# Mamba stage of a decoder layer: the side work of the next item placed at other states, half of delta times x on VectorE

## The reference, cut to what matters

```
xz = x @ in_w.T;  xb, z = split(xz)                       # 512 channels each
xb = silu(causal_conv(xb, 4 taps) + cb)
delta, Bm, Cm = split(xb @ xp_w.T)                         # ranks 16, 16, 16
delta = softplus(delta @ dt_w.T + dt_b)
mi  = delta[..., None] * Bm[:, :, None, :] * xb[..., None]
v_t = 0.6 * v_{t-1} + mi_t                                 # per channel and state
h_t = exp(delta_t * -exp(a_log)) * h_{t-1} + v_t
y   = sum over the 16 states of h * Cm;  y = (y + dp * xb) * silu(z)
x   = x + y @ out_w.T
```

## Time and profile before

| | |
|---|---|
| median of three runs | 1560.0 us |
| profiled execution | 1560.36 us, of which the span of the instructions is 1558.9 us |
| Mamba block (first to last scan) | 80.5 to 982.0 us of the span |
| TensorE, ScalarE, VectorE, GpSimd busy, share of the span | 88%, 58%, 68%, 59% |

### The profile page before, as it was taken

How to read it: one execution, slowest core, us unless ns; L and a number is a source line. 1 busy time by engine, 2 the same in 40 slices (tenths; PEclk the granted TensorE clock), 3 DMA queues, 4 the chain that set the end, 5 groups by cost and what they waited for, 6 DMA issues and landing times.

```text
span 1558.9 us, 46788 instructions
## 1 busy us (share of the span) xinstructions
PE 1372.9 (88%) x20442; PEld 975.9 (63%) x20442; DVE 1066.0 (68%) x1347; ACT 908.8 (58%) x1365; POOL 921.2 (59%) x802
## 2 busy tenths in 40 slices
PE   4679799999899899899899886878989887999997
PEld 2357577777677677667677775533444343499996
DVE  4189898798689688788788786577676771422223
ACT  3658567777767667767666765116555655434440
POOL 1159888989979969969969986530303000035541
PEclk8689999999999999999999998969999999999999
DMA  4102212222212212221221344370414100612225
GB/s 134 49 28 85 83 65 75 85 83 96 84 71 84 84 57 84 84 72 69 87 81 70 138 128 125 76 149 1 84 39 85 24 1 15 264 47 69 68 66 179
DMA packets 41497, 127.26 MB, mean 82 GB/s; under 512 B 8784, under 2 KB 21584, under 8 KB 32848
## 3 DMA queue, kind: packets, MB, share of 16 engines
q1 hardware_dynamic: 34736, 108.27, 21.4%
q0 software_dynamic: 6048, 14.95, 3.6%
q10 hardware_dynamic: 512, 1.05, 0.4%
HBM read 97.90 MB, written 9.57 MB: 69 GB/s over the span
## 4 chain that ended last, share of the span: by engine, by line
PE 59%; DVE 20%; issue 10%; ACT 4%; POOL 4%; DMA 2%; DVEq 0%; SPq 0%; ACTq 0%; POOLq 0%
PE psum L631 12%; DVE hst L783 9%; PE psum L610 8%; PE psum L1710 4%; PE psum L1722 4%; PE psum L1298 4%; PE psum L515 3%; POOL hst L987 3%; PE psum L601 3%; DVE overlay L679 2%; PE psum L1280 2%; DVE w_early L783 2%; PE psum L1652 2%; PE psum L1264 2%; DVE nmax L1419 2%
## 5 line engine op out<-in xcount | busy, mean ns | idle before, releaser
L987 POOL TENSOR_TENSOR hst<-hst,cb 128x512 f32<-128x512 f32 x399 | 513.5, 1306 | 125.7 <-DVE hst L783 110.3
L783 DVE TENSOR_TENSOR_SCAN hst<-dA,psum 128x512 f32<-128x512 f32 x399 | 467.1, 1204 | 140.7 <-PE psum L631 140.4
L610 PE MATMUL psum<-ident,hst 128*128 128x128 f32 x1596 | 236.5, 282 | 15.6 <-POOL hst L987 12.7
L610 PEld LDWEIGHTS psum<-ident,hst 128*128 128x128 f32 x1596 | 174.2, 141 | 66.3 <-issue 25.4
L923 ACT ACTIVATE dA<-delta,alog 128x512 f32<-128x512 f32 x256 | 177.0, 718 | 63.1 <-DVE hst L783 43.9
L923 ACT ACTIVATE dA<-xres,alog 128x512 f32<-128x512 f32 x256 | 176.1, 718 | 47.8 <-DVE hst L783 35.6
L1419 DVE TENSOR_REDUCE nmax<-psum 128x2 f32<-128x1024 f32 x128 | 154.6, 1220 | 55.3 <-PE psum L1264 54.8
L1348 ACT ACTIVATE pT<-psum 128x1024 f32<-128x1024 f32 x128 | 128.0, 1024 | 102.9 <-PE psum L1284 79.3
L631 PE MATMUL psum<-filt,c_early 64*64 64x86 f32 (+1 forms) x6144 | 147.2, 241 | 32.8 <-DVE hst L783 23.6
L631 PEld LDWEIGHTS psum<-filt,c_early 64*64 64x64 f32 x6144 | 126.6, 136 | 68.8 <-issue 39.9
L631 PE MATMUL psum<-filt,uT 64*64 64x86 f32 (+1 forms) x6144 | 144.8, 238 | 23.8 <-DVE hst L783 14.6
(11 more groups left out here) (236 smaller groups left out, 2130.5 us busy)
## 6 DMA issues: line engine op xcount, KB each, us to landing
cb<-c_rows SPq DMA_DIRECT2D x64, 1024.0 KB, 4.7
qk_first<-w_early SPq DMA_DIRECT2D x64, 64.0 KB, 2.4
qk<-part SPq DMA_DIRECT2D x64, 64.0 KB, 2.7
w_up<-up_dram SPq DMA_DIRECT2D x8, 512.0 KB, 7.3
w_down<-down_dram SPq DMA_DIRECT2D x8, 512.0 KB, 12.9
w_up<-y_choice SPq DMA_DIRECT2D x8, 512.0 KB, 6.9
qk<-part POOLq DMA_DIRECT2D x48, 64.0 KB, 5.2
qk_first<-part SPq DMA_DIRECT2D x40, 64.0 KB, 2.4
```

What stands on the lines that cost most here:

```text
L610: m = pe.matmul(psum[:, Y0 + et % EP, t * P:(t + 1) * P], hst(i)[:, t * P:(t + 1) * P], ident[:], start=n == 0 and t == 0, stop=n == NSTAT ...
L783: dve.tensor_tensor_scan(hst(i), a, v, 0.0, ALU.mult, ALU.add).then_inc(scan_done, 1)
L987: pool.tensor_tensor(h, h, cb[:, q % 2, state_of(i)[1] % GN, :], ALU.mult).then_inc(g_done, 1)
```

## The change

What moves, by step (in the front of items 2 to 7 unless said otherwise; the front of item 1 keeps its `p`, and item 7 its `bo`):

| side | before | after |
|---|---|---|
| `p` 0 to 3 | 8, 10, 12, 14 | 5, 8, 11, 14 |
| `bo` 0 to 3 | 15, 17, 18, 19 | 19, 25, 29, 34 |
| `z` 0 to 3 (also item 1) | 35, 36, 37, 38 | 38, 41, 45, 58 |
| `u` 0 to 3 (also item 1) | 36 to 39, all on POOL | 36 to 39, tiles 1 and 3 on DVE |
| `gate` 0 and 1 | 40, 42 | 50, 57 |
| filters of the next item | POOL at steps 34, 38, ... 62 | 41, 47, 53, 59, and 1, 7, 13, 19 of the next item |

```diff
-                p_at = (8, 10, 12, 14) if k > 1 else range(start + 5, start + 5 + ET)
+                p_at = (5, 8, 11, 14) if k > 1 else range(start + 5, start + 5 + ET)
...
-                    put(36 + m, "pool", "u", m)
-                    put(35 + m, "pe", "z", m)
-                    put(36 + m, "act", "z", m)
+                    put(36 + m, "dve" if m % 2 else "pool", "u", m)
+                    put((38, 41, 45, 58)[m], "pe", "z", m)
+                    put((38, 41, 45, 58)[m] + 1, "act", "z", m)
...
-                    s = s + 1 if at == "last" else ((17, 19, 21, 23) if at == NI - 1 else (15, 17, 18, 19))[t]
+                    s = s + 1 if at == "last" else ((17, 19, 21, 23) if at == NI - 1 else (19, 25, 29, 34))[t]
...
-                    steps["pool"].setdefault((k, s + 3), []).append((k, "gate", e))
+                    steps["pool"].setdefault((k, (50, 57)[e]), []).append((k, "gate", e))
...
-                    pe.wait_ge(u_done, ET // 2 if k == 0 else ET * k + ET // 2)
-                    if k == 0:
-                        pe.wait_ge(u_first, ET // 2)
+                    pe.wait_ge(u_done, ET // 2 * (k + 1))
+                    pe.wait_ge(u_first, ET // 2 * (k + 1))
...
-            FEARLY = 3
+            FEARLY, PACE0, PACE = 3, 41, 6
...
-                    if k + 1 < NI and r >= EP * NSTATE and r % (2 * EP) == 2:
-                        pool_filter(NPAIRS * (k + 1) + (r - EP * NSTATE) // (2 * EP))
+                    if i >= PACE0 and (i - PACE0) % TILES % PACE == 0 and (i - PACE0) % TILES < PACE * NPAIRS and (i - PACE0) // TILES + 1 < NI:
+                        pool_filter(NPAIRS * ((i - PACE0) // TILES + 1) + (i - PACE0) % TILES // PACE)
```

More of the change, by code:

```diff
@@ L1048, in sp_mamba @@
                     sp_c_load(NUSE * k + 5)
+                    sp_c_load(NUSE * k + 6)
+                    sp_c_load(NUSE * k + 7)
                     if k == B - 2:
@@ L1056, in sp_mamba @@
                         sp.dma_start(b_qk[:], d["b_qk"]).then_inc(ld_bqk, 16)
-                    sp_c_load(NUSE * k + 6)
-                    sp_c_load(NUSE * k + 7)
                     if k == NI - 1:
```

## The result

Four runs of the changed kernel took 1590.4 to 1605.7 us, median 1599.5; the kernel before, beside them, 1560.1. The ratio is 1.025 (95% interval 1.020 to 1.030): **slower by 39 us**, where 1592 had been forecast, in a range of 1548 to 1614. The profiled execution took 1605.66 us, 45.3 more than the one of before. By items (first scan to first scan) these divide into +0.3 ahead of item 0, +3.5 in item 0, +10.1 in item 1, +26.2 in items 2 to 6, +2.2 in item 7 and +3.0 behind the Mamba block. Items 1 to 6 are where the prediction had its sum (+31.8); they gave +36.4. The profiled execution is thus 13.5 us above the 1592 forecast for it: 4.6 of them in items 1 to 6, 5.7 in items 0 and 7, 3.3 around the Mamba block.

A forecast was written before the change was run, and what follows sets the result against it. An item is TensorE's work plus its still time, except steps 0 to 15, where VectorE rules. Items grow to 118.1 us: +22.0 for items 2 to 6, +9.8 for item 1, together +31.8 on 1560.4, giving 1592 us, range 1548 to 1614.

The forecast's parts named there:

- Steps 0 to 15: 29.3 becomes 31.4 us: `p` 0 at step 5 waits 1.3 us for VectorE's second `xn` copy, delaying v 6 and scan 6.
- Steps 16 to 35: Two stretches: 16.8 becomes 12.0 us as two `bo` leave; 16.5 becomes 19.7 as three `bo` come and one `z` goes.
- Steps 36 to 51: 30.6 becomes 33.5 us: same work, but new waits of 4.1 us, with a kept gap 4.7 against 1.8.
- The 2.2 us put on v 42: Steps 36 to 51: v 42 takes the bank of v 40 and waits 2.2 us for scan 41 and `xd` 0.
- `u` at 1.0: Steps 36 to 41: each `u` on VectorE takes 1.0 us, between 0.66 and 1.64; ends -0.7 and +1.3 us per item.
- Steps 52 to 63: 20.8 becomes 21.5 us: `z` 3 at step 58 needs 1.73 us, but a turn has only 1.14 us idle.
- item 1, +9.8: Item 1 gets the same bank pattern as the others, so it goes from 108.3 to 118.1 us.
- The loop: Steps 52 to 63: v and scans wait on each other's banks, a pair every 3.71 us, TensorE idle 1.14 us a turn.
- Items 0 and 7: First and last items: no `p` and no `bo` move there, so nothing changes, within 3 us.
- Rival A: Levelling pays: TensorE finds its banks free, v 42 to v 50 start without idle time, -22 us, 1538 us; chance 0.20.
- Rival D: VectorE and GpSimd block each other in steps 36 to 51: some 4.3 us more per item, 1619 us; no chance stated.
- SP: Loads of C go ahead of weights that wait for `z` 3; cost nothing, `w_in` having 15 or more us of cover.

The follow-up runs named there:

- experiment 5: Kernel before with only `p` moved to steps 5, 8, 11, 14: 1565.2 us (1.005 to the kernel before).
- experiment 8: Kernel before, nothing moved, another bank rule (a v pair takes only banks 0-1, 2-3 or 4-5; sides follow): 1537.1 us (0.986).
- experiment 3: Changed kernel with all four `u` back on GpSimd: 1581.5 us (1.016 to the kernel before).
- experiment 7: Changed kernel with `p` back at 8, 10, 12, 14 and all `u` on GpSimd: 1571.1 us (1.007 to the kernel before).
- experiment 10: Kernel before with `bo`, `z`, gates and filters moved, `p` and `u` as before, plus the other bank rule: 1526.9 us (0.979).
- experiment 11: Changed kernel with VectorE's two `u` at steps 39 and 40 instead of 37 and 39: 1593.6 us (1.021 to the kernel before).
- experiment 1: Changed kernel with the four `p` back at steps 8, 10, 12, 14: 1583.6 us (1.018 to the kernel before).
- experiment 2: Changed kernel with only `p` 0 moved back, to step 7, behind the v of step 6: 1588.2 us (1.018 to the kernel before).
- experiment 9: Changed kernel with the other bank rule (a v pair takes only banks 0-1, 2-3 or 4-5; sides follow): 1558.1 us (0.999 to the kernel before).
- experiment 4: Kernel before with only the GpSimd part (two `u` on VectorE, later gates, spread filters) and SP's new load order: 1558.7 us (1.001).
- experiment 6: Kernel before with only `bo` moved to steps 19, 25, 29, 34: 1569.6 us (1.006 to the kernel before).

## Why the prediction was right, point by point

**Steps 0 to 15, +2.1 (measured +2.44).** Right in every row: TensorE's 1.29 us ahead of `p` 0 (1.3 forecast), VectorE's 2.12 ahead of scan 6 (2.1). Undoing `p`, and undoing `p` 0 alone, gave it back: shown.

**Steps 16 to 35, -1.6 (measured 16.8 + 16.5 to 12.2 + 19.8, -1.2).** Work that moves from one full stretch of TensorE to the next. Right. The forecast's 19.7 does not quite follow from its terms: 16.5 + 3.5 is 20.0, v 28 waits 0.8 more (it did, 0.80), and the idle time before was only 0.7.

**Steps 36 to 51, +2.9 (measured +2.7).** The sum was right and its make-up only partly. Of the waits, v 44 (1.1), v 48 and v 50 (0.4 each) came as written. The 2.2 us put on v 42 came as 1.18 ahead of `bt` 1, which the list did not have, and 1.20 ahead of v 42. From scan 36 to scan 40 VectorE took 636.22 - 627.69 = 8.53 us, 8.4 forecast, but with other addends: `u` at 0.66, the lower end, and one `max` at 1.76. The forecast's `u` at 1.0 stood by chance for 0.66 plus a share of that `max`: its 8.4 leaves 0.63 for each `max`, less than any in the earlier trace rows.

**Steps 52 to 63, +0.7 (measured +0.55), and item 1, +9.8 (measured +10.1).** Right. The loop comes from the banks: shown by the count of experiment 5 and by experiment 8. `z` 3 uses one turn's idle time, and four waits of 1.14 to 1.17 are left.

**Items 0 and 7, "nothing, within 3 us".** This step failed: +5.7 together. The text looked at `p` and `bo` only; `z`, `u` and the filters move there as well. In item 0, steps 36 to 51 took 34.8 us before, 30.4 with the GpSimd part alone, and 30.1 to 30.9 in the kernels with `z` moved where `u` was back or apart from `max` (experiments 3, 7, 10, 11). In the changed kernel and in experiments 1, 2 and 9 they take 33.4 to 33.9. There TensorE waits 2.77 us for VectorE (1.07 in experiment 3), and right behind that wait the granted clock falls, 0.51 from 154.10 to 157.50 us, so that a `z` takes 3.51 us instead of 1.88. PE, changed kernel, item 0:

```profile
153.73 0.76 PE L594 MATMUL psum<-ident,xraw 128*128 128x128 f32 x4 [2.77 <-DVE hst L782]
154.29 3.51 PE L515 MATMUL psum<-overlay,w_early 128*128 128x512 f32 x4
```

The rest of item 0's +3.5 lies in steps 52 to 63 (+4.1), partly at a lower clock (last section). In item 7 the spread filters cost 2 to 3 us (experiment 4). The other 3.0 us behind the Mamba block lie in code that is the same; that stretch took 572.5 to 582.0 us in the profiles, so this is scatter.

**Rival A, levelling pays.** Wrong for this change, but not empty: v 42 to v 50 did start without idle time in experiment 10, when both the waits for VectorE and the bank waits had been taken out, and there it paid.

**Rival D, the shared port.** Right in kind, 1.1 us per item instead of 4.3. Against the kernel before it is less still, because one `max` per item was held up there too (1.50 us in item 4): the three behind scan 36 took 2.82 us together, now 3.08. It is the rule of the Trainium skill, page SBUF — State Buffer, section Who interferes with whom: where a VectorE instruction with two SBUF inputs meets one of GpSimd that reads SBUF, the second to issue is blocked until the first has finished. The rows agree: VectorE's `max` ended 0.55 us behind the end of GpSimd's `u` (630.57 + 1.75 = 632.32 and 631.11 + 1.76 = 632.87; in experiment 11, 626.60 and 627.15). The first `u` at 0.66 while GpSimd's took 1.75 is the same rule the other way round.

**SP.** The late loads were costed at nothing. In item 3 this term was too small: steps 0 to 15 are 1.2 us longer there than in its neighbours. TensorE stops for 1.02 us inside the v of step 2, with no wait that the profile shows.

```profile
446.05 0.96 PE L630 MATMUL psum<-filt,uT 64*64 64x86 f32 x37 [1.02 <-issue]
```

The packets of the DMA queues show what comes ahead of it. From 437.3 to 444.0 us two loads of 1 MB each ran, one of them `w_in`. A packet of the instruction queue (16 KB) began at 443.73, as they ended, and TensorE went on at 446.05, 2.3 us later. The same holds for nearly all such stops: in the 13 traces TensorE stopped 43 times for over 0.3 us without a wait between 195 and 930 us, and 42 times it went on 2.2 to 2.7 us after such a packet had begun (one comes every 6.6 us or so). The gap of 1.09 us in the earlier trace rows is one of them, so is the v of step 46 in experiment 6: there 1 MB ran from 389.34 to 393.05, the packet began at 393.05, and the v went on at 395.21. Stops inside the v of step 2 or 6 of item 3 stand in all eight kernels with `z` moved, where `w_in` is loaded just then, and in none of the five others. That TensorE's code arrives late behind the bulk load is what these times point to; no experiment moved the load alone.

## What to carry to other kernels

When buffers are dealt out in program order, a moved instruction changes whom every later one waits for: work out the new predecessors item by item (not for one item) before costing a move, and try a better dealing rule before moving work, since here the rule alone gave 1.4% and the change without it took 2.5%. An input that comes from the engine which rules a stretch must not be waited for ahead of the work which feeds that engine. An engine that is busy throughout is no bound as long as the wait list shows nobody waiting for it; relieving it was worth nothing in items 2 to 6 here.

## What was not expected of the hardware

What a VectorE instruction with both inputs in SBUF takes follows from GpSimd here. In items 1 to 6 of the changed kernel all 36 `max` and `u` of VectorE began while an instruction of GpSimd ran, and each ended 0.55 to 0.59 us behind the end of that instruction. Most began 0.07 to 0.09 us ahead of that end, behind a scan, and took 0.66. The `max` behind a `u` began 1.21 us ahead of it, since GpSimd had got in between, and took 1.76. In experiment 6 five `max` began beside no GpSimd instruction; they took 0.67.

TensorE's granted clock fell after a short stand inside a busy stretch, but not each time. In experiment 11 TensorE stood still for 2.04 or 2.05 us ahead of v 42 in each of items 1 to 6; behind it the clock fell in items 1, 4 and 6 and stayed at 1.00 (2.4 GHz) in items 2, 3 and 5. In item 4 it was 0.57 over the next 4 us (for the most part the lower of its levels, 1.2 GHz). The price is the difference of these items above, 0.5 to 0.8 us. Busy time of the engines, in the same columns as above, from 511 us (item 3) and from 629 us (item 4):

```profile
511.00:515.00 4.00, 2.90 (x93) 2.50 (x85) 2.99 (x3) 1.08 (x3) 4.00 (x4) 1.00 0.70 262
```

```profile
629.00:633.00 4.00, 3.80 (x80) 3.24 (x75) 2.99 (x3) 0.95 (x3) 4.00 (x5) 0.57 0.72 262
```

In the changed kernel's item 0 the last stretch (179.50 to 206.95 us) ran at a clock of 0.81, before (179.90 to 203.20) at 0.85. The runs of the changed kernel spread over 15 us; those of the kernel before, taken beside the experiments, spread over up to 13, so that is not the change's own doing.
